# First attention's last outputs done inside the first iterations of the layers, and the layers' weight splits at other places

## The reference, cut to what matters

```python
def _L0_attn_ref(x, P_q, P_k, P_v, P_o):
    Q = jnp.einsum('bmd,hdk->bhmk', x, P_q)
    K = jnp.einsum('bmd,hdk->bhmk', x, P_k)
    V = jnp.einsum('bmd,hdv->bhmv', x, P_v)
    logits = jnp.einsum('bhmk,bhnk->bhmn', Q, K) * math.sqrt(D_K)
    causal = jnp.tril(jnp.ones((m, m), dtype=bool))
    logits = jnp.where(causal[None, None], logits, -jnp.inf)
    key_weights = jax.nn.softmax(logits, axis=-1)
    o = jnp.einsum('bhmm,bhmv->bhmv', key_weights, V)
    y = jnp.einsum('bhmv,hdv->bmd', o, P_o)
...
    for i in range(DEPTH):       # DEPTH = 6
        x = attn_layer(shift_tokens(x), Wqkv[i], q_scale[i], k_scale[i], Wo[i]) + x
        x = ffn_layer(shift_tokens(x), ln_g[i], ln_b[i], W1[i], b1[i], W2[i], b2[i]) + x
...
    # ffn_layer: layer norm with gain g and bias bln, then
    hg = xn @ W1 + b1
    a, gate = jnp.split(hg, 2, -1)
    return a * jax.nn.gelu(gate, approximate=False) @ W2 + b2
...
x = _layernorm(x + _L0_attn_ref(x, P_q, P_k, P_v, P_o))
x = _layernorm(x + _L0_ffn_ref(x, ...))
```

## Time and profile before

| | |
|---|---|
| median of 3 runs | 3686.01 us (3685.73 to 3690.58) |
| the profiled execution | 3685.71 us |
| its span, first to last instruction | 3683.8 us |
| mean granted TensorE clock | 0.996 |
| busy: PE, PEld | 3569.0 us (97%), 3039.1 us (82%) |
| busy: DVE, ACT, POOL | 3130.2 us (85%), 3362.8 us (91%), 2745.0 us (75%) |
| DMA | 132.71 MB, mean 36 GB/s |

### The profile page before, as it was taken

The page is one execution under the profiler, slowest core; times in us unless marked ns, Lnnn a source line. Parts: engine busy times, 40 slices in busy tenths (PEclk is TensorE's granted clock), DMA queues, the critical chain, the costliest instruction groups (busy, mean ns, idle before and its releaser), DMA issues.

```text
span 3683.8 us, 133067 instructions
## 1 busy us (share of the span) xinstructions
PE 3569.0 (97%) x47348; PEld 3039.1 (82%) x47348; DVE 3130.2 (85%) x7019; ACT 3362.8 (91%) x10923; POOL 2745.0 (75%) x2060
## 2 busy tenths in 40 slices
PE   8999989999999999999999999999999999999998
PEld 5666678888888888888888888888888888888887
DVE  8999888888888788888888888878888888888897
ACT  8999779999999899999999999899998999999996
POOL 0111288888888888788788888888888888888884
PEclk9999999999999999999999999999999999999999
DMA  2000011111111111111111111111111111111111
GB/s 101 7 16 7 10 44 37 36 28 37 42 42 39 32 33 39 38 44 38 33 32 38 40 45 34 32 29 41 49 34 36 30 33 44 33 35 38 41 35 38
DMA packets 165015, 132.71 MB, mean 36 GB/s; under 512 B 113933, under 2 KB 124813, under 8 KB 164109
## 3 DMA queue, kind: packets, MB, share of 16 engines
q1 hardware_dynamic: 164365, 124.19, 13.8%
HBM read 25.84 MB, written 4.19 MB: 8 GB/s over the span
## 4 chain that ended last, share of the span: by engine, by line
PE 75%; DVE 5%; ACT 4%; issue 3%; DVEq 0%; ACTq 0%; POOLq 0%; POOL 0%
PE bank L1067 10%; PE bank L1023 10%; PE bank L1103 8%; PE bank L1048 8%; PE bank L1087 7%; PE bank L985 4%; PE bank L986 4%; PE bank L987 4%; PE bank L946 4%; PE bank L1080 3%; PE bank L919 2%; PE bank L921 2%; ACT a_E L1395 2%; PE bank L920 2%; PE bank L999 2%
## 5 line engine op out<-in xcount | busy, mean ns | idle before, releaser
L1498 POOL TENSOR_TENSOR a_rn<-a_ssqc,a_minus_half 128x16 f32<-128x16 f32 x384 | 1113.3, 2899 | 509.4 <-DVE a_ssqc L1689 499.6
L1395 ACT ACTIVATE a_E<-bank,a_negmax 128x96 f32<-128x96 f32 x3072 | 1012.9, 362 | 23.2 <-DVE a_negmax L1638 22.6
L1519 POOL TENSOR_TENSOR a_r<-a_u,a_rn 128x512 f32<-128x512 f32 x768 | 788.2, 1046 | 0.6
L1506 POOL TENSOR_TENSOR a_PN<-a_E,a_erec 128x384 f32<-128x384 f32 x768 | 739.6, 983 | 11.7 <-PE bank L1048 8.2
L1395 ACT ACTIVATION_READ_ACCUMULATOR a_E<-bank,a_negmax 128x1 f32 x3072 | 707.0, 230 | 0.0
L1378 ACT ACTIVATE a_QK<-bank 128x512 f32<-128x512 f32 x768 | 466.8, 608 | 130.2 <-PE bank L1023 130.1
L1651 DVE TENSOR_TENSOR a_u<-bank,a_rot_c 128x512 f32<-128x512 f32 x768 | 522.0, 680 | 2.4 <-ACT a_sq L1371 2.4
L1661 DVE TENSOR_TENSOR a_v<-bank,a_rot_s 128x512 f32<-128x512 f32 x768 | 522.7, 681 | 0.0
L1371 ACT ACTIVATE a_sq<-bank 128x512 f32<-128x512 f32 x768 | 482.5, 628 | 43.3 <-PE bank L987 13.5
L1023 PE MATMUL bank<-ident,a_r 128*128 128x128 f32 x3072 | 483.4, 280 | 18.3 <-DVE a_bias L1624 11.9
L1356 ACT ACTIVATE a_PT<-bank 128x512 f32<-128x512 f32 x758 | 479.2, 632 | 19.2 <-PE bank L1048 15.2
(11 more groups left out here) (182 smaller groups left out, 8092.6 us busy)
## 6 DMA issues: line engine op xcount, KB each, us to landing
a_V_even<-a_V_odd SPq DMA_DIRECT2D x384, 128.0 KB, 2.3
a_V_even<-a_V_odd SPq DMA_DIRECT2D x192, 64.0 KB, 2.1
a_raw<-in_qkv SPq DMA_DIRECT2D x20, 384.0 KB, 3.6
a_x_sh<-X SPq DMA_DIRECT2D x48, 128.0 KB
a_V_even<-a_V_odd SPq DMA_DIRECT2D x192, 32.0 KB, 2.0
a_x_sh<-X SPq DMA_DIRECT2D x48, 127.0 KB
a_f_sh<-X SPq DMA_DIRECT2D x47, 128.0 KB
a_f_sh<-X SPq DMA_DIRECT2D x47, 127.0 KB
```

Of the source, the lines that this page charges most:

```text
L1395: ins = act.activation(E[:, s.par, k, :], scores[:, i % 2, col:col + KW], ACT.Exp, bias=negmax[:, s.par, k:k + 1], accum_out=esum[:, s.par ...
L1498: pool.tensor_tensor(rn[:, a.par, :], ssqc[:, a.par, :], minus_half[:, :], ALU.pow).then_inc(S["rn"], 1)
L1506: pool.tensor_tensor(PN[:, s.par, 2 * hp:2 * hp + 2, :].rearrange("p i (b k) -> p i b k", b=2)[:, :, :, 0:KW], spread(E[:, s.par, half, :] ...
L1519: pool.tensor_tensor(heads(r[:, a.par, half]), heads(u[:, a.par, half]), rn[:, a.par, mm * 2 * HG:(mm + 1) * 2 * HG].unsqueeze(2).to_broad ...
```

## The change

In the first attention, batch 7's weighing, transposes, copies, projections, sum and norm, and batch 6's last projection, sum and norm leave the drain, which has 5 steps for 16 (none on POOL but one). VectorE weighs pieces 0 and 1 at the block's end, POOL weighs 2 to 7 at the beginning of the layers' block, in place in V (`weigh_values`). Values of the pieces 4 and 6 use another bank. In iteration 0, TensorE does the transposes and projections (`late_outputs`, `late_projection`) at the end of the cycles of pairs 0 to 3 and at the start of pair 4's, ScalarE copies at the start of pairs 1 to 4, VectorE sums at the start and at (0, 5). Statistics and norms of the two batches stand in iteration 1, with the power on POOL at (1, 2) and (1, 4); SyncE keeps their X0 at (1, 6) and (2, 1).

The block of pads is gone; its memsets stand in the layers' cycles (PN on POOL at the end of pair 1). To make room, buffers of the layers share space with those of the first attention (`late`); the loads of raw weights in iteration 1 wait for the sum. W1's first preparation moves from iteration 0 to 1. In every preparation the biases stand behind the first cosines of pair 1, and w1l in pair 4; w1h is made in two halves at pairs 0 and 1. The low halves of the QKV weights are made at (7, 4), (7, 5), (8, 2), (8, 4), for (7, 2), (7, 4), (7, 6), (8, 0) before; of the high halves the last moves from (8, 0) to (8, 1).

```diff
-F_BANKS = 5
+F_BANKS, F_DRAIN = 5, 5
...
+        def value_bank(batch, pos):
+
+            return p_y if batch == NB - 1 and pos in (4, 6) else p_vt
...
-                every_step(dve, step, STEPS)
+                every_step(dve, step, F_DRAIN)
+                dve.wait_ge(all_ready, NB)
+                for piece in range(2):
+                    dve.wait_ge(v_out, (NB - 1) * 8 + piece + 1)
+                    weigh_values(dve, V, prob_all, piece).then_inc(S["d_o"], 1)
+
+def weigh_values(engine, V, prob_all, u):
+
+    i, half = divmod(u, 2)
+    piece = V[:, i, half * T:half * T + T].rearrange("p (h f) -> p h f", f=DH)
+    return engine.tensor_tensor(piece, piece, prob_all[:, i, 8 * half:8 * half + 8].unsqueeze(2).to_broadcast([P, 8, DH]), ALU.mult)
...
+P_SPLIT = ((0, 2), (0, 4), (0, 6), (1, 1))
+P_LOW = ((0, 4), (0, 5), (1, 2), (1, 4))
...
 def prepared(n):
 
-    if n == 0:
+    if n == 1:
         return 0
...
-def layer_pads(nc, ctx, A):
...
+    def split_at(n, p, places=P_SPLIT):
+
+        for g, (first, place) in enumerate(places):
+            layer = (n + 1 - first) // NB
+            if (n + 1 - first) % NB == 0 and p == place and 0 < layer < DEPTH:
+                return layer, g
+        return None
...
+            def late_outputs(u):
+                i, half = divmod(u, 2)
+                pe.wait_ge(S["d_o"], u + 1)
+                ge(pe, S["d_ot_out"], u - 1)
+                for c in range(4):
+                    ins = pe.transpose(p_late[u % 2][:, c * P:(c + 1) * P], late["V"][:, i, half * T + c * P:half * T + (c + 1) * P], ident[:, :])
+                ins.then_inc(S["d_ot"], 1)
...
+            def late_pieces(n, p):
+                if n == 0 and p < 4:
+                    for u in (2 * p, 2 * p + 1):
+                        if p:
+                            pe.wait_ge(S["d_ot_out"], u - 1)
+                            if u == 2:
+                                pe.wait_ge(S["d_sum"], 1)
+                            late_projection(u - 2)
+                        late_outputs(u)
+
+            def late_end(n, p):
+                if (n, p) == (0, 4):
+                    pe.wait_ge(S["d_ot_out"], 7)
+                    late_projection(6)
+                    pe.wait_ge(S["d_ot_out"], 8)
+                    late_projection(7).then_inc(S["d_z"], 1)
...
             def cycle(n, p):
                 s = pair_at(n, p, LAG_S)
+                late_end(n, p)
                 project(n, p, 0)
...
                 values(n, p)
+                late_pieces(n, p)
...
             transpose_x(0)
+            late_projection(7).then_inc(S["d_z"], 1)
             every_iteration(pe, cycle)
...
-                if p == 0:
-                    split_up(n)
-                split_qkv(n, p)
+                if p < 2:
+                    split_up(n, p)
+                split = split_at(n, p)
+                if split:
+                    split_qkv(*split)
...
+                if (n, p) == (0, 1):
+                    pool.memset(PN[:, :, :, :], 0.0).then_inc(S["pads"], 1)
...
                 cosines(n, p, 0)
+                if p == P_BIAS:
+                    biases(n)
                 if p == P_TURN:
+                    split_qkv(n, p)
                     turned(n)
...
                 norms(n, p)
-                if p == P_BIAS:
-                    split_up(n)
-                    biases(n)
                 cosines(n, p, 1)
...
                 reciprocals(s, 0)
                 if p == 0:
                     stats(n)
+                if p == P_GATES:
+                    split_qkv(n, p)
+                    split_up(n)
                 if p == P_GELU:
+                    split_qkv(n, p)
                     feed_forward_out(n)
...
-                split_qkv(n, p)
+                if (n, p) == (0, 5):
+                    late_sum(NB - 1, 2)
...
+                if (n, p) in ((1, 3), (1, 6)):
+                    late_norm(NB - 3 + p // 3, p // 3)
+                if (n, p) in ((1, 1), (1, 3)):
+                    late_stats(NB - 2 + p // 2, 1 + p // 2)
```

202 lines of the change are left out of this document (120 added, 82 removed).

## The result

The changed kernel takes 3644.49 us at the median of 4 runs (3641.75 to 3645.64), for 3685.99 before; the ratio is 0.9883, interval 0.9866 to 0.9901. The prediction was 3649, range 3638 to 3662.

A forecast was written before the change was run, and what follows sets the result against it. TensorE, with 75% of the chain of waits, was taken to bound the kernel. 3685.7 -16.8 (start of layers) -16.8 (biases) -3.0 (boundaries) = 3649 us, with 3638 to 3662 to hold 8 times in 10.

The forecast's parts named there:

- Term 1: Start of the layers, iterations 0 and 1: first transposes 21.1 us earlier, part given back; -16.8 us (-21 to -11).
- Term 3: Boundaries of layers, iterations 8, 16, 24, 32, 40: moved QKV splits gain 0.6 each, -3.0 us (-8.5 to +5).
- A: Iterations 0 and 1: the fill eats much of the earlier start, price 11 us, time 3660; chance 0.10.
- B: Preparations of W1: the bias wait goes only in part, or clock falls continue; time 3660; chance 0.08.
- C: Five boundaries: VectorE's split at pair 2 is blocked at the ports by POOL's power; 10 us, 3659; chance 0.05.
- E: Boundaries of layers get worse through a split in a pair without cover; +8 over the forecast, 3657; chance 0.05.
- -0.6 +0.2 +1.5 +0.8: Iteration 0, us: TensorE's clock kept, POOL's fill, TensorE's added work in the fill, its wait for ScalarE's copies in (0, 4).
- late end: Cycle (0, 4): TensorE begins by waiting for two copies that ScalarE does first; +0.8 us (0 to 1.5).
- Iteration 1 ... +1.2 (0 to 2.5): Iteration 1: VectorE's added statistics and norms, partly covered by 1.13 us idle a pair, cost +1.2 us; shift matmuls +1.25.
- Term 2: Iterations 4, 12, 20, 28, 36: five bias waits go, -11.9, and three clock falls, -4.9; -16.8 us (-18 to -9).
- the split at pair 2 has only some tenths of cover and costs 1.1: Boundary iterations: VectorE's remaining split, ahead of the gate's products, costs 1.1 of the 1.7 us attributed to splits.
- Rival D: From the start's gap through iteration 1: TensorE stays at its lower clock level, 57 us more, 3706; chance 0.02.

The follow-up runs named there:

- the third experiment: The changed kernel with the biases put back behind the sum of squares, their old place, and the w1l split left in pair 4; 3653.26 us.

## Why the prediction was right, and where it was wrong by step

The direction, the three places and the size of the whole were right: -41.5 us for -37 forecast. But the sum was better than its terms, and that is luck: Term 1 brought 4.2 us less than forecast and Term 3 brought 10.3 more, and the two stand against each other. By the two profiles the whole is -43.9.

Of the rivals, A came in part, with 7.0 us given back in iterations 0 and 1. B did not come, as no bias wait is left. C did not show either: VectorE's split in pair 2 took 1.39 us (at 971.58) and not 2.90; but it ran beside POOL's weighing of PN and products and not beside a power, so this row does not test it. Nor did E, as the boundaries got shorter.

**Term 1** was to bring -16.8 and brought -12.6. The 21.1 us for the start came as 21.6, and the mechanism is right: the block's end behind the weighing, the clock kept, a wait of TensorE for ScalarE in (0, 4). It rests on the timelines; no run takes the shorter drain, the missing block of pads or the split weighing by itself. Two of its numbers were off against each other: the weighings ended at 442.63 and not 442.2, as the last copy of probabilities came 0.46 later, and from there TensorE began after 0.33 us, where the block change was put at 1.21.

Iteration 0 grew by 3.1; its terms (-0.6 +0.2 +1.5 +0.8) make +1.9. The wait of the late end was 1.67 us for 0.8. A wait that the prediction does not name grew as well: TensorE's wait for exponentials, 1.47 us in the profile of before at 496.28, is 2.22 at 477.74.

The step "Iteration 1 ... +1.2 (0 to 2.5)" failed. The statistics and norms cost 2.64 in iteration 1 and 1.9 in iteration 2, shown by leaving them out. I had netted VectorE's work against 1.13 us of idle time a pair; the idle time is there because VectorE waits for exponentials (8.4 us in 8 waits of iteration 1 before), and most of it is still there behind the added work (5.9 us in 7 waits): only 2.5 us of the 6.1 that VectorE does more went into it. In iteration 2 the norm at (1, 6) stands ahead of a_xl in VectorE's row, so all of it is on TensorE's path; the row order named it and I did not follow it past the iteration's end. It cost 2.15 us and not 1.1, as its operations ran beside POOL's.

**Term 2** was to bring -16.8 and brought -16.6, iterations of 66.6 as forecast. The bias part is shown twice: the part alone gives it, and with the biases back 1.5 of the 2.35 return. That the clock's falls belong to the wait is borne out by its removal; that they belonged to iterations 12, 28 and 36 was chance.

**Term 3** was to bring -3.0 and brought -13.3, outside its own bounds. (The upper bound of +5 doesn't follow either: nothing gained and five splits of 1.58 make +7.9.) Two steps failed. The first is mis-sized: "the split at pair 2 has only some tenths of cover and costs 1.1". With this split moved behind the reciprocals the iteration is 0.2 shorter; and from before to after iteration 8 lost 1.8 us (68.29 to 66.51), all of the 1.7 that the prediction gave to the splits. In the profile of before these are two waits of iteration 8, for VectorE's a_xl and a_v; neither the changed kernel nor the one with the places alone has them:

```profile
966.53 0.63 PE L1023 MATMUL bank<-ident,a_r 128*128 128x128 f32 x4 [0.93 <-DVE a_xl L1574]
...
983.64 0.47 PE L985 MATMUL bank<-a_wh,a_xh 128*128 128x512 f32 x1 [0.99 <-DVE a_v L1661]
```

The second is a term that was missing: 0.9 us in each of the iterations 7, 15, 23, 31 and 39. It is a wait of TensorE ahead of line 946 that the profile puts down to "issue", and the prediction has no word of it:

```profile
947.22 2.92 PE L946 MATMUL bank<-w_w,a_h 128*128 128x128 f32 x24 [0.92 <-issue]
```

With the places alone changed it is gone. What makes the 1.2 us that are left of iteration 8 stays open. 0.2 is VectorE's split in pair 2. ScalarE's split may hold more of it, as it and VectorE's hide each other (above). The prediction's 1.3 for the rotations is neither shown nor refuted: they stand where they stood, no run leaves them out, and neither was VectorE's split in pair 4 or the first use of the new weights tried alone.

**The clock.** Rival D (the lower level for whole iterations) did not come. But short falls are part of this kernel's scatter: kernels with the same row at a place show one in one run and not in another. At the start of iteration 2, two windows of the changed kernel, the wait and behind it:

```profile
555.61:557.61 2.00, 0.00 (x0) 0.00 (x0) 2.00 (x4) 0.59 (x4) 1.83 (x2) 1.00 0.06 13
559.61:561.61 2.00, 2.00 (x36) 1.65 (x36) 1.65 (x5) 1.89 (x10) 0.95 (x1) 1.00 0.12 26
```

The same two of the kernel with the projections behind the scores, whose row is the same there:

```profile
557.01:559.01 2.00, 0.00 (x0) 0.00 (x0) 2.00 (x4) 0.59 (x4) 1.83 (x2) 1.00 0.06 13
561.01:563.01 2.00, 2.00 (x8) 1.65 (x7) 1.65 (x5) 1.00 (x4) 0.95 (x1) 0.50 0.12 26
```

TensorE is idle throughout the first window in both, and then works at 1.00 in the one and 0.50 in the other; the iteration takes 65.60 and 67.23. Counted over the profiles, by the lengths: behind the 2.1 us at the start of iteration 2, 4 of 8 fell (65.6 to 65.7, or 67.2 to 67.3); behind the 2.2 to 2.4 in iteration 0, 5 of 11; behind the 2.0 ahead of the end, 7 of 14 (130.0 to 130.4, or 131.4 to 131.8), before's among them and not after's, which is the last row of the table; behind the 2.35 bias waits, 3 of 5 and 4 of 5. Behind the 1.5 us waits of the third experiment none of 6 fell. But in the fill of the kernel before the clock was 0.50 in 481 to 483, behind a wait of 1.56 us that ended at 480.10, so the shorter waits are not safe everywhere. A fall costs 1.0 to 1.8 us. So, as an estimate from these counts (behind waits of 2 us and more 23 of 43 fell) and this cost, a wait of 2 us at such a place costs nearly 3 at the mean. Chance, and not the change, is 1.8 of the 43.9 us between the two profiles; and the profiled run of the changed kernel is the one of its four with clock 1.000, the others have 0.999 and are 2.2 to 3.9 us longer.

## What to carry to other kernels

Compare the lengths of a kernel's repeated stretches, not totals: with a period that repeats to 0.1 us, a single profile showed terms of 0.2 us where five iterations agreed, and two opposite errors that the total had hidden. When work moves into an engine with idle time, ask what that idle time waits for; it is cover only if the added work stands where the engine waits, and whatever follows in its row within the iteration, and into the next, is late by the rest. Work that is split off to run "at the end of a cycle" should stand where its engine is idle and nothing that TensorE needs comes next: the same splits cost 2.6 us a layer more at the ends of the cycles (7, 2), (7, 4), (7, 6) and (8, 0) than inside those of (7, 4), (7, 5), (8, 2) and (8, 4). How much of this is the pair and how much the place inside it was not tried. And where two engines each have extra work in the same stretch, taking one away can show nothing: each may hide the other.
